# Retention and a mixture of experts on one core: drains, seam and setup reordered, and the expert stage's normalising moved to ScalarE

## What is computed

```python
def _L0_ffn_ref(src, ...):                 # 16 heads of 8, 4 experts with 512 hidden units
    q, k, v = src @ Wq + bq, src @ Wk + bk, src @ Wv + bv      # split into heads
    probs = jax.nn.softmax(jnp.einsum('bqhd,bkhd->bhqk', q, k) * scale)
    attn = jnp.einsum('bhqk,bkhd->bqhd', probs, v) @ Wo + bo
    x = _layer_norm(src + attn, ln1_g, ln1_b)
    expert_idx = jnp.remainder(jnp.floor(x @ router_w + router_b), N_EXPERTS)
    for e in range(N_EXPERTS):
        y = jax.nn.relu(x @ W1[e] + b1[e]) @ W2[e] + b2[e]
        ff_out = ff_out + jnp.where((expert_idx == e)[..., None], y, 0.0)
    return _layer_norm(x + ff_out, ln2_g, ln2_b)
# _L0_attn_ref: retention, 8 heads: rotary q and k, scores times a causal decay mask, values,
# a norm over each head, times silu(x @ W_g), times W_proj
x = x + 0.5 * _L0_ffn_ref(_layernorm(x), ...)
x = x + _L0_attn_ref(_layernorm(x), ...)
x = x + 0.5 * _L0_ffn_ref(_layernorm(x), ...)
```

## Time and profile before

| | |
|---|---|
| median of three runs | 1092.86 us (1092.46 to 1098.92) |
| the profiled execution | 1100.55 us |
| its span, first to last instruction | 1098.7 us |
| setup and attention phase 0 with its drain | 0 to 334 us |
| expert stage 0 | 334 to 430 us |
| retention | 430 to 686 us |
| attention phase 1 with its drain | 686 to 999 us |
| expert stage 1 | 999 to 1099 us |
| TensorE / VectorE / ScalarE / GpSimd busy | 901.3 / 778.2 / 655.8 / 623.4 us |

### The profile page before, as it was taken

How to read it: one execution, slowest core, us unless ns; L and a number is a source line. 1 busy time by engine, 2 the same in 40 slices (tenths; PEclk the granted TensorE clock), 3 DMA queues, 4 the chain that set the end, 5 groups by cost and what they waited for, 6 DMA issues and landing times. The chain is left out here.

```text
span 1098.7 us, 26792 instructions
## 1 busy us (share of the span) xinstructions
PE 901.3 (82%) x8603; PEld 665.1 (61%) x8603; DVE 778.2 (71%) x1930; ACT 655.8 (60%) x1326; POOL 623.4 (57%) x921
## 2 busy tenths in 40 slices
PE   5798999999946883788888888799999999955984
PEld 3565666666626782566666566566666666634883
DVE  4787888888844885455555655478888888843886
ACT  2587888888824441344343444498888888832552
POOL 4144756657552665366666667326657566562665
PEclk9998999999967997799999999599999999966998
DMA  9985980000007772000000000000000000006781
GB/s 301 411 309 74 400 353 19 14 14 19 17 34 225 221 213 81 11 1 1 0 0 0 0 0 1 1 1 12 11 19 19 10 19 14 16 20 189 210 240 54
DMA packets 41557, 97.69 MB, mean 89 GB/s; under 512 B 5224, under 2 KB 24958, under 8 KB 36876
## 3 DMA queue, kind: packets, MB, share of 16 engines
q1 hardware_dynamic: 35980, 84.16, 23.7%
q0 software_dynamic: 5504, 12.63, 3.2%
HBM read 44.68 MB, written 53.13 MB: 89 GB/s over the span
## 5 line engine op out<-in xcount | busy, mean ns | idle before, releaser
L1215 DVE TENSOR_REDUCE mx<-duo 128x4 fp32r<-128x1024 f32 x256 | 312.3, 1220 | 75.5 <-PE duo L524 70.7
L947 ACT ACTIVATE probs<-duo 128x1024 f32<-128x1024 f32 x256 | 263.4, 1029 | 58.2 <-PE duo L530 55.1
L524 PE MATMUL duo<-stacks 32*128 32x256 f32 x1024 | 133.3, 338 | 35.2 <-DVE mx L1215 29.6
L577 PE MATMUL duo<-probs,v_st 128*32 128x256 f32 x2048 | 142.4, 397 | 0.0
L530 PE MATMUL duo<-q_st,stacks 32*128 32x256 f32 x1024 | 131.3, 335 | 4.7 <-ACT probs L947 4.7
L1418 DVE TENSOR_TENSOR ret<-duo,dm 128x768 f32<-128x768 f32 x64 | 61.2, 956 | 103.8 <-PE duo L766 99.9
L524 PEld LDWEIGHTS duo<-stacks 32*128 32x128 f32 x1024 | 80.5, 191 | 70.4 <-issue 40.9
L1571 POOL TENSOR_TENSOR a_ln<-mv_ln,eps_ln 128x2 f32<-128x2 f32 x32 | 6.3, 197 | 154.5 <-DVE mv_ln L1182 154.5
L517 PE MATMUL duo<-qk_hi,sel_r 128*128 128x256 f32 x256 | 82.9, 344 | 7.4 <-DVE qk_lo L1204 7.4
L658 PE MATMUL duo<-w,probs 128*128 x608 | 76.6, 279 | 7.7 <-issue 4.3
L530 PEld LDWEIGHTS duo<-q_st,stacks 32*128 32x128 f32 x1024 | 78.0, 188 | 6.1 <-issue 3.2
(11 more groups left out here) (209 smaller groups left out, 2453.8 us busy)
## 6 DMA issues: line engine op xcount, KB each, us to landing
x_sorted<-ret SPq DMA_DIRECT2D x2, 17476.0 KB, 53.4
wbuf<-w_pack SPq DMA_DIRECT2D x38, 512.0 KB, 3.4
ret<-x_sorted SPq DMA_DIRECT2D x22, 257.0 KB, 3.8
stacks<-x_sorted SPq DMA_DIRECT2D x12, 257.0 KB, 4.1
wside<-w_pack SPq DMA_DIRECT2D x38, 66.0 KB, 3.7
w_pack<-wbuf SPq DMA_DIRECT2D x2, 1024.0 KB, 8.1
decay_rows<-prow SPq DMA_DIRECT2D x1, 1536.0 KB
probs<-x_sorted SPq DMA_DIRECT2D x4, 257.0 KB, 3.7
```

Source lines behind the costliest of these rows:

```text
L524: return pe.matmul(score_bank[h % 2][:, t * SEQ:(t + 1) * SEQ], q_st[r:r + 32, g, t * P:(t + 1) * P], k_st[r:r + 32, g, :], start=True, st ...
L577: last = pe.matmul(pv_bank[32 * j:32 * j + 32, cols], v_st[:, t, h, :], probs[:, h % RING, t, :], start=(t == 0), stop=(t == TT - 1))
L947: act.activation(probs[:, h % RING:h % RING + 2, :, :], prob_duo[:].rearrange("p (n t q) -> p n t q", n=2, t=TT), ACT.Exp, scale=SCALE).th ...
L1215: dve.tensor_reduce(rows, score_duo[:].rearrange("p (n t k) -> p n t k", n=2, t=TT), AX.X, ALU.max, negate=True).then_inc(max_done, 1)
```

## The change

- **Experts.** finish is split. VectorE's moments(k-2) computes unit (the root) and, new, drop (minus mean times root); ScalarE's normal(k-2) then computes z * unit + drop, two activations of 128x128; VectorE's finish(k-2) multiplies by g2 and adds the residual, each one instruction of 128x256. VectorE's order is split_x, moments, add_ffn, finish. yo_ready counts once a tile.
- **Loads.** Rows are loaded four tiles ahead, the biases have a ring of 5 and a semaphore and a load_side of their own. The first row number and the first expert are read before the scatter has landed.
- **Drain.** In the iteration after the last batch the second scores go by turns to prob_bank and score_bank. The last batch's layer norm is ended by VectorE (last_x1) with GpSimd's root, and GpSimd does own_row ahead of it.
- **Seam.** Pairs 1 and 2 of the first attention iteration now stand together on TensorE and ScalarE; the last outputs of retention come later on TensorE; on VectorE sum_squares(15) comes before pair 1. The table of exp and log is loaded ahead of retention(15).
- **Setup.** Tiles 2 and 3 of x are loaded ahead of W1; parts 2 to 13 of later_setup move to iteration 1.

```diff
-            sp.dma_start(xs[:, 2:BATCH], xv[:, 2:BATCH]).then_inc(ld_xs, 16)
+            sp.dma_start(xs[:, 2:4], xv[:, 2:4]).then_inc(ld_xs, 16)
+            sp.dma_start(xs[:, 4:BATCH], xv[:, 4:BATCH]).then_inc(ld_xr, 16)
...
+                def load_side(k, e=None):
+                    n = first + k
+                    wait(sp, h_ready, 4 * (n - WS_RING + 1))
+                    wait(sp, xb_ready, n - WS_RING + 1)
+                    e = expert_of(k) if e is None else e
+                    sp.dma_start(wside[:, n % WS_RING, :], w_pack[bass.ds(e, 1), :, 2 * DFF:PACK].rearrange("e p n -> p (e n)")).then_inc(ws_in[n % WS_RING], 16)
...
                 for k in range(TILES):
+                    if k + 4 < TILES:
+                        load_x(k + 4)
                     if k + 2 < TILES:
                         load_w(k + 2)
                     if k + 3 < TILES:
-                        load_x(k + 3)
+                        load_side(k + 3)
...
+                    if turned == 1:
+                        pe.wait_ge(max_done, (b2 + 1) * (NH // 2))
+                    wait(pe, exp_done, b2 * (NH // 2) + h2 // 2 - (1 if turned else 0))
+                banks = score_bank if turned is not None and turned % 2 else prob_bank
...
             attend(BATCH, slots(0, 0))
             retain(BATCH, slots(2, 3))
-            attend(BATCH, slots(1, 1))
-            retain(BATCH, slots(4, 7))
-            attend(BATCH, slots(2, 4))
-            retain(BATCH + 1)
+            attend(BATCH, slots(1, 2))
+            retain(BATCH, slots(4, 4))
+            attend(BATCH, slots(3, 3))
+            retain(BATCH, slots(5, 7))
+            retain(BATCH + 1, slots(0, 4))
+            attend(BATCH, slots(4, 4))
+            retain(BATCH + 1, slots(5, 7))
             attend(BATCH, slots(5, 7))
...
+                def normal(k):
+                    n = first + k
+                    act.wait_ge(ln2, n * 8 + 8)
+                    wait(act, yo_ready, n - 1)
+                    for t in range(TT):
+                        last = act.activation(zn[:, n % 2, t, :], z[:, n % 3, t, :], ACT.Identity, bias=drop[:, n % 2, t:t + 1], scale=unit[:, n % 2, t:t + 1])
+                    last.then_inc(zn_ready, 1)
...
                         relu(k)
+                    if k >= 2:
+                        normal(k - 2)
...
+            def last_x1(b, base):
+
+                s = ln_scratch["ln1"]
+                dve.wait_ge(ln1, b * 8 + 4)
+                for t in range(TT):
+                    dve.scalar_tensor_tensor(n1[:, t, :], y1[:, t, :], s["mv"][:, t, 0:1], g1_b, ALU.subtract, ALU.mult).then_inc(last_scaled, 1)
+                dve.wait_ge(ln1, b * 8 + 8)
+                for t in range(TT):
+                    dve.wait_ge(last_scaled, 2 * (b // BATCH) + t + 1)
+                    dve.scalar_tensor_tensor(x1_all[:, b - base, t, :], n1[:, t, :], s["rstd"][:, t:t + 1], b1_b, ALU.mult, ALU.add).then_inc(x1_ready, 1)
...
                 def finish(k):
                     n = first + k
...
+                    dve.wait_ge(zn_ready, n + 1)
+                    dve.tensor_tensor(zn[:, n % 2], zn[:, n % 2], g2_b.unsqueeze(1).to_broadcast([P, TT, P]), ALU.mult).then_inc(zg_ready, 1)
                     wait(dve, yo_out[n % 3], 32 * (n // 3))
...
+                    dve.tensor_tensor(yo[:, n % 3], zn[:, n % 2], xt[n % XT_RING][:, :, DM:2 * DM], ALU.add).then_inc(yo_ready, 1)
...
                         split_x(k + 1)
+                    if 2 <= k < TILES + 2:
+                        moments(k - 2)
+                    if 1 <= k <= TILES:
+                        add_ffn(k - 1)
                     if k >= 2:
                         finish(k - 2)
-                    if 1 <= k <= TILES:
-                        add_ffn(k - 1)
...
-                        if isinstance(i, int) and i == 0 and 1 <= p:
-                            later_setup(2 * p - 2)
-                            later_setup(2 * p - 1)
+                        if isinstance(i, int) and i == 0 and p == 1:
+                            later_setup(0)
+                            later_setup(1)
...
+                        if isinstance(i, int) and i == 1 and 1 <= p <= 6:
+                            later_setup(2 * p)
+                            later_setup(2 * p + 1)
...
             retain(BATCH - 1, slots(7, 7))
-            attend(BATCH, slots(1, 1))
             retain(BATCH, slots(0, 4))
-            attend(BATCH, slots(2, 2))
+            attend(BATCH, slots(1, 2))
+            retain(BATCH, slots(7, 7))
+            attend(BATCH, slots(3, 3))
             retain(BATCH, slots(5, 6))
-            attend(BATCH, slots(3, 3))
-            retain(BATCH, slots(7, 7))
             attend(BATCH, slots(4, 4))
             retain(BATCH + 1)
             attend(BATCH, slots(5, 7))
...
                     if live(i - 2, base):
...
+                    if is_last(i - 2, base):
+                        own_row(i - 2, base)
+                        rstd(i - 2, "ln1", 3)
```

120 lines of the change are left out of this document (69 added, 51 removed).

## The result

The changed kernel takes 1068.06 us in the median of four executions (1064.49 to 1070.79), the kernel before beside it 1095.89: a ratio of 0.974, 95% interval 0.969 to 0.980. Taken again later, six executions against eleven, the ratio is 0.973 (0.970 to 0.977). Forecast were 1054.2 and 38.7 us of gain against the profiled execution; the time lies inside the range, 14 us above the point. The two profiled executions are 36.1 us apart, the medians about 28: the profiled one of before was its slowest, the one of after its fastest.

What follows compares the result with a forecast made beforehand. VectorE, stalled by GpSimd, was taken to set the expert tile's pace, 4.33 us against TensorE's 3.43. Experts 15.0, loads 1.8, setup 4.5, seam 6.0 and drains 11.4 sum to 38.7; from median 1092.86, 1054.2 us, range 1037 to 1071.

Steps and rivals of the forecast that it cites:

- 7.5 a stage: Expert stages: tiles at 3.88 us instead of 4.33 give 8.1, less 0.6 for the last tile; 15.0 in all.
- 0.9 from the loads: Expert stage start: second rows issued 1.4 us earlier, third weights some 0.5 later; gain 0.9 a stage, 1.8 in all.
- The term 0.7 x 4.07: Expert tile: a share of about 0.7 of VectorE's last additions is held by GpSimd, making those tiles take 4.07 us.
- rival B's 3.43: Expert stages: VectorE's addition always slips in before GpSimd's, so tiles take TensorE's 3.43 us; total 1038.0, chance 0.17.
- what the prediction named as a way to fail: Expert stages: SP's longer round, some 0.5 us more a tile, might make TensorE wait for weights.
- The prediction's test of the rule: Expert tile: if whoever starts first keeps the port, VectorE's addition begun at 2.8 ends before GpSimd's at 3.1.
- the held case: Expert tile: VectorE's addition starts at 2.8, is held to the end of GpSimd's, and ends at 4.07 us.
- the 0.5 that I guessed: Expert stage start: third weights, behind one more row load and bias load, come some 0.5 us later.
- 4.2 against 4.5: Setup: VectorE's wait for the last small load and TensorE's idle leave iteration 0; gain 4.5 us, bounds 1 and 6.
- the exps (3.0): Each drain: exps take scores from two banks by turns, so the copy of the values comes 3.0 us earlier, bounds 1.3 and 3.6.
- last_x1 (2.65): Each drain: VectorE ends the last layer norm instead of waiting for GpSimd's normalising; gain 2.65 us, counted as 2.7.
- 6.0 forecast: Seam between retention and second attention: reordering moves pairs 2 and 5 earlier; gain 6.0 us, ends 3.8 and 7.

Runs made afterwards that it cites:

- no_b2: The changed kernel without GpSimd's additions of b2 in the expert stages, VectorE adding the rows directly (output not the reference's); 1062.15 us, ratio 0.962.
- lean_start: The changed kernel with a shorter SP round, plus first expert weights loaded before the last scatter lands and first two row loads back to back; 1054.12 us, ratio 0.959.
- warm: lean_start plus 12 identity transposes by TensorE into an unused bank while it waits for the first rows; 1055.69 us, ratio 0.961.

## Why the prediction was right, and where it was not

- **Experts: mechanism right, two sizes off against each other.** Forecast 7.5 a stage with 0.9 from the loads, measured 8.2 and 9.6 for both. The term 0.7 x 4.07 was mis-sized: 2 of 19 additions are held to the end (4 in stage 0), not 0.7 of them, since 7 start 0.34 to 0.43 before GpSimd's and pay 0.25 to 0.38 instead of the 0.84 of the sum, and 8 meet none. The stall is 0.24 a tile (0.31 in stage 0), and VectorE no longer sets the pace. By this alone rival B's 3.43 was due. Against it stands what the prediction named as a way to fail and costed at nothing: SP's round, 3.42 us, makes TensorE wait for weights. Hence 3.72. That the errors cancelled to within 1 us a stage is luck. The Trainium skill (SBUF — State Buffer, "Who interferes with whom") calls the ports that VectorE and GpSimd share an exclusive lock, and says, of VectorE's two-port modes, that whoever issues first has them for the whole instruction. The row at 1006.56 disagrees by the recorded starts, as VectorE starts first and still takes 0.80 instead of 0.42, and GpSimd's addition, begun while it ran, takes 0.96. The inference in the same section of the Trainium skill, that descriptor generation and such an addition use different interfaces, agrees with all 19 additions of no_b2. The prediction's test of the rule has a slip: an addition of 0.43 begun at 2.8 ends at 3.23, not before GpSimd's at 3.1. In the traces one placed so, 0.30 ahead, takes 1.33 (stage 0, at 390.07), so the held case was costed right and only its share was not.
- **Loads: the step failed.** I gave them 0.9 a stage by the second rows' wait. That wait fell as said (3.11 to 1.73), but the third weights came 3.3 us later against the 0.5 that I guessed, and the first result 1.1 to 1.4 later instead of 0.9 earlier. What I left out of the sum altogether was the ring from SP's wait for GpSimd's addition to TensorE's rows: without the new loads the new finish is worth 1.9 to 3.5 us a stage, and beside it the new loads 5.2 to 7.3.
- **ScalarE's activations** take 0.49 us each (38 of them, 0.477 to 0.507) and a pair 0.88, not 0.33 and 0.66; with 60.40 us of 89 ScalarE is still not the bound, as said.
- **Drains: right in mechanism, both terms small.** 3.9 for the exps (3.0) and 3.6 for last_x1 (2.65), in all 7.5 and 6.5 against 5.7. The router came 2.45 us after its moments. In the time of the whole the drains show as 11 us where they are added and as 5 where they are taken out.
- **Setup: right in its stretch**, 4.2 against 4.5 in the first two profiles, though the eleven with the new setup average 295.3 at the last maximum of phase 0 and the three with the old one 298.4, 3.1 apart and with ranges that touch; the time of the whole doesn't show it. VectorE no longer waits for a DMA in iteration 0, and iteration 1 took the 21.1 that were foreseen as some 20.
- **Seam: right in the mean, by luck in part** (5.9 over eleven profiles, 6.0 forecast). It is 6.7 to 8.0 where the clock is mostly up and 2.9 in the profile that I compared; the forecast had no term for the clock. The stalls moved on to pair 4, which the prediction had named as a way to fail: in that profile VectorE waits there for TensorE, which works at the low clock (0.50) through transposes and projection of retention's last batches ahead of the scores. Of the middle as a whole 2.9 is left in the mean.
- **The point, 1054.2, was 14 us low.** Subtracting from the median what was summed in a trace took the sum for 38.7; the traces agree with 37. Only 28 to 30 arrive in the medians. It is not that the clock got worse, as the granted clock of the middle is 0.94 in both profiles: 37 was measured between the slowest execution of the one and the fastest of the other.

## What to carry to other kernels

When one engine is relieved, lay the rounds of all others beside the new pace, the queue that only issues DMAs among them: here five stood within a few tenths of 3.4 us, and a round as long as the tile never catches up after a hiccup. Look for rings: a wait that stands ahead of other loads in a queue couples them all to its releaser, and the two halves of this change were worth at most 3.6 us a stage each, and 8 to 10 together. And where the clock wanders, judge an edit by its own stretch in the trace and by many executions, not by the difference of two spans.

The lean kernel, one register read less a tile and the third weights earlier, beats both: 1056.66 us, 0.958 of the kernel before.

## What the runs showed of the hardware

- The same program's middle lasted 526.3 to 538.3 us by TensorE's granted clock alone (means 0.96 and 0.93), with the other engines' busy times equal to 0.5 us. The low level, 1.2 GHz against 2.4, showed in both drains of all 14 profiles, for 34.1 to 37.5 us with the old drains and 17.1 to 27.3 with the new, and in retention and the seam now at one place, now at another.
- Two SBUF inputs on VectorE against GpSimd's addition: both are stretched when they overlap (0.80 for 0.42 and 0.96 for 0.66), and what VectorE pays is not settled by which is recorded first: 1.32 where it started 0.27 us before GpSimd's (995.65 against 995.92), 0.80 where it started 0.43 before, 0.75 to 0.77 where it started 0.5 behind. In the 38 additions of the changed kernel's first profile the six long ones start 0.21 to 0.33 ahead; in its second one at 0.34 is long as well. In the kernel before, an instruction of 0.34 begun 0.48 ahead was held each time, though free it would have been over before GpSimd's recorded start.
- The first rows, 257 KB, were in use 2.84 us after their issue with the 512 KB of weights issued behind them, and 3.85 after it with the weights issued ahead. Over all profiles it is 2.68 to 3.02 in the 24 stage starts of the first kind, and 3.54 to 4.00 in the 4 of the second (`lean_start`, `warm`).
